# The main loop's patch transforms: once per two steps with 512 columns, in place of once per step with 256

## The reference

```
xn     = layernorm(x)                                 # 16 channels
hidden = xn @ w_hidden                                # 192 channels
qkv    = conv3x3(hidden, w_qkv, SAME)                 # 192 channels, split into q, k, v of 64
out    = irfft2(rfft2(patches(q)) * rfft2(patches(k)))  # patches of 8 x 8 pixels
out    = v * layernorm(out)                           # over 64 channels
out    = out @ w_out + x                              # 16 channels
```

## Time and profile before

| | |
|---|---|
| median of three runs | 236.66 us (236.47 to 239.24) |
| the profiled execution's own time | 237.58 us |
| its span, first to last instruction | 235.8 us |
| PE busy | 219.5 us (93%) |
| DVE busy | 159.4 us (68%) |
| ACT busy | 133.8 us (57%) |
| POOL busy | 76.9 us (33%) |
| mean granted TensorE clock | 0.993 |

### The profile page before, as it was taken

One profiled execution on the slowest core, in us unless ns is written; L12 is line 12 of the kernel. 1 busy time (PEld: TensorE's weight loads), 2 busy tenths in 40 slices (PEclk: granted clock), 3 DMA queues, 4 the chain that ended last, 5 costly groups with the idle time before them and its releaser, 6 DMA issues.

```text
span 235.8 us, 4977 instructions
## 1 busy us (share of the span) xinstructions
PE 219.5 (93%) x1926; PEld 144.1 (61%) x1926; DVE 159.4 (68%) x301; ACT 133.8 (57%) x286; POOL 76.9 (33%) x70
## 2 busy tenths in 40 slices
PE   7989999895989899779999999999999999999983
PEld 3359434772447557268676676767676777767561
DVE  3995123567743983646489978678786889677793
ACT  3366475323174754344678666667667576766533
POOL 1635500012300000000051766426654364549730
PEclk9999999999799999999999999999999999999999
DMA  6920000000000018989997479999950000000001
GB/s 215 329 70 7 16 8 4 20 3 0 4 0 0 0 64 190 223 193 194 201 197 151 141 137 191 182 179 202 191 118 0 3 24 25 0 1 3 22 0 67
DMA packets 22647, 21.07 MB, mean 89 GB/s; under 512 B 1898, under 2 KB 21242, under 8 KB 22522
## 3 DMA queue, kind: packets, MB, share of 16 engines
q1 hardware_dynamic: 22352, 20.62, 43.0%
q10 hardware_dynamic: 272, 0.14, 0.3%
HBM read 16.58 MB, written 4.02 MB: 87 GB/s over the span
## 4 chain that ended last, share of the span: by engine, by line
PE 68%; DVE 16%; ACT 6%; DMA 6%; issue 2%; SPq 1%; DVEq 0%; ACTq 0%
PE psum L1229 22%; PE psum L1240 13%; PE psum L1250 7%; PE psum L1102 5%; PE psum L1175 4%; PE psum L1260 3%; DMA arena<-parts 3%; DVE xc L781 2%; PE psum L1080 2%; DVE sq L793 2%; PE psum L1090 2%; PE psum L1063 2%; DMA parts<-tr 2%; DVE st L787 2%; PE psum L1286 2%
## 5 line engine op out<-in xcount | busy, mean ns | idle before, releaser
L1229 PE MATMUL psum<-wc,tile 128*128 128x192 f32 (+1 forms) x384 | 59.4, 305 | 3.5 <-ACT tile L378 1.9
L1229 PEld LDWEIGHTS psum<-wc,tile 128*128 128x128 f32 (+1 forms) x384 | 51.4, 159 | 13.7 <-issue 7.8
L557 POOL TENSOR_TENSOR zp<-zp,ln 128x512 f32<-128x512 f32 x14 | 17.8, 1274 | 100.6 <-DVE zp L937 100.6
L916 DVE TENSOR_TENSOR arena<-psum,arena 128x512 f32<-128x512 f32 x32 | 22.1, 691 | 27.5 <-ACT arena L716 27.2
L378 DVE COPY tile<-arena 128x256 f32<-128x256 f32 x64 | 25.1, 435 | 2.1 <-DMA arena<-parts 2.1
L1175 PE MATMUL psum<-arena,wdw 102*128 102x512 f32 x48 | 23.5, 631 | 0.9 <-ACT arena L339 0.9
L716 ACT COPY arena<-psum 128x512 f32<-128x512 f32 x32 | 18.8, 586 | 9.0 <-PE psum L1240 9.0
L1250 PE MATMUL psum<-arena,km 128*64 128x256 f32 x128 | 20.9, 405 | 0.2 <-DVE arena L916 0.2
L709 ACT COPY spec<-psum 128x768 f32<-128x768 f32 x16 | 12.8, 799 | 12.7 <-PE psum L1229 12.7
L558 POOL TENSOR_TENSOR zp<-zp,ln 128x512 f32<-128x512 f32 x14 | 17.8, 1271 | 1.1
L1240 PE MATMUL psum<-spec,km 64*128 64x256 f32 x128 | 18.2, 402 | 0.0
(11 more groups left out here) (129 smaller groups left out, 373.1 us busy)
## 6 DMA issues: line engine op xcount, KB each, us to landing
arena<-padded SPq DMA_DIRECT2D x16, 393.0 KB, 9.8
arena<-parts SPq DMA_DIRECT2D x16, 196.5 KB, 9.7
arena<-padded SPq DMA_DIRECT2D x8, 262.0 KB, 10.4
parts<-tr SPq DMA_DIRECT2D x12, 115.5 KB
wq<-w_qkv SPq DMA_DIRECT2D x1, 1296.0 KB, 11.9
padded<-tr SPq DMA_DIRECT2D x4, 264.0 KB, 3.9
arena<-parts SPq DMA_DIRECT2D x8, 131.0 KB, 9.6
out<-xt SPq DMA_DIRECT2D x8, 128.0 KB, 1.7
```

The source lines that it names most:

```text
L557: pool_link(pool.tensor_tensor(y, y, along(0), ALU.mult))
L916: dve.tensor_tensor(pr[:, m % 2], f_half(m, 0), kh[:, m % 2], ALU.mult).then_inc(prod, 1)
L1229: last = mm(bank[a][:, HID * h:HID * h + HID], stationary[:, n % 2, 2 * h + a, :], moving[:, :], start=first and h == 0, stop=not first, s ...
```

## The change

The transforms forward and back are done once a pair, with 512 columns a matmul. `forward(i)` fills four banks, 2 to 5: first the two k matmuls, with a signal of their own (`fk_mm`), then the two q matmuls (`f_mm`). `k_out` copies 1024 columns and `product` multiplies 1024, both with one buffer in place of two. The inverse has bank 6 alone in place of banks 4 and 5 by turns, and `turn` and `unit` share bank 7. The last pair stays in halves, as before, on banks 0 to 3. The orders of all three loops are written anew over pairs s: PE runs convolution 2s, forward of pair s-1, unit, convolution 2s+1, turn, inverse of pair s-1. On DVE `finish` stands right behind `o_scale`, with the next `gather` and then `o_sum` behind it; on ACT `o_square` stands ahead of `conv_out(2s)`, and `k_out` behind it. The parts of the second half of the images are split at s = 1 and 2.

```diff
-        kh = spare[:, 0:1024].rearrange("p (i q n) -> p i q n", i=2, q=2)
-        pr = spare[:, 1024:2048].rearrange("p (i q n) -> p i q n", i=2, q=2)
+        kh, pr = spare[:, 0:1024], spare[:, 1024:2048]
...
         def o_bank(i):
-            return bank[4 + i % 2]
+            return bank[6 if i < 15 else 4]
...
         def yt_bank(i):
-            return bank[6 if i < 15 else 0]
+            return bank[7 if i < 15 else 0]
...
-            def k_out(m):
-                act.wait_ge(f_mm, m + 1)
-                if m >= 2:
-                    act.wait_ge(prod, m - 1)
-                act.copy(kh[:, m % 2], f_half(m, 1)).then_inc(k_ev, 1)
+            def k_out(i):
+                act.wait_ge(fk_mm, i + 1)
+                if i >= 1:
+                    act.wait_ge(prod, i)
+                act.copy(kh, psum[:, 2048:3072]).then_inc(k_ev, 1)
...
             gather9(0)
-            for n in range(32):
-                if n + 1 < 32:
-                    gather9(n + 1)
-                if n in (6, 7):
+            for s in range(16):
+                gather9(2 * s + 1)
+                if s >= 2:
+                    o_square(s - 2)
+                conv_out(2 * s)
+                if s >= 1:
+                    k_out(s - 1)
+                if s in (1, 2):
                     for b2 in range(2):
-                        part(1, n - 6, b2)
...
+                        part(1, s - 1, b2)
+                if s < 15:
+                    gather9(2 * s + 2)
+                if s >= 2:
+                    root(s - 2)
+                u = unit_after(s - 4)
+                if u is not None:
                     unit_out(u)
+                conv_out(2 * s + 1)
+                if 3 <= s < 15:
+                    turned(s - 3)
+
+            k_out_half(0)
+            k_out_half(1)
...
+            def product(i):
+                dve.wait_ge(k_ev, i + 1)
+                dve.wait_ge(f_mm, i + 1)
+                if i >= 1:
+                    dve.wait_ge(o_mm, i)
+                dve.tensor_tensor(pr, psum[:, 1024:2048], kh, ALU.mult).then_inc(prod, 1)
...
             gather(0)
...
+            for s in range(16):
+                gather(2 * s + 1)
+                if s == 1:
+                    bordered(1)
+                if s >= 2:
+                    o_sum(s - 2)
+                    o_centre(s - 2)
+                if s == 0:
                     normalise(2, 1, xc[:, 1])
...
+                if s < 15:
+                    gather(2 * s + 2)
+                if s >= 2:
+                    o_variance(s - 2)
+                if s >= 1:
+                    product(s - 1)
+                if s in (1, 2):
+                    split(1, s - 1)
+                if s >= 2:
+                    o_scale(s - 2, o_norm)
+                u = unit_after(s - 4)
+                if u is not None and u < 5:
                     finish(u)
...
+            def forward(i):
+                pe.wait_ge(qkv_ev, 2 * i + 2)
+                pe.wait_ge(x2_done, 8)
+                if i >= 1:
+                    pe.wait_ge(prod, i)
+                for part, name, signal in ((1, "fk", fk_mm), (0, "fq", f_mm)):
+                    for q in range(2):
+                        rows = slice(64 * q, 64 * q + 64)
+                        src = qkv[i % 4][rows, :, :, CH * part:CH * part + CH].rearrange("p e t c -> p (e t) c")
+                        last = mm(bank[2 + 2 * part + q][:, :], const(name)[rows], src, start=True, stop=True)
+                    last.then_inc(signal, 1)
...
+            def inverse(i):
+                pe.wait_ge(prod, i + 1)
+                if i == 0:
+                    pe.wait_ge(tr_ev, 4)
+                else:
+                    pe.wait_ge(o_centred, i)
                 for q in range(2):
-                    last = mm(o_bank(i)[64 * q:64 * q + 64, 256 * e:256 * e + 256], const("inv4"), pr[:, m % 2, q, :], start=True, stop=True)
+                    last = mm(o_bank(i)[64 * q:64 * q + 64, :], const("inv4"), pr[:, 512 * q:512 * q + 512], start=True, stop=True)
+                last.then_inc(o_mm, 1)
...
                     pe.wait_ge(yt_ev, i)
+                    if unit_after(i - 1) is not None:
+                        pe.wait_ge(pj_ev, unit_after(i - 1) + 1)
...
+            for s in range(16):
+                conv(2 * s)
+                if s >= 1:
+                    forward(s - 1)
+                u = unit_after(s - 4)
+                if u is not None:
+                    unit(u)
+                if s == 1:
                     channel_major(1)
...
+                conv(2 * s + 1)
+                if 3 <= s < 15:
+                    turn(s - 3)
+                if s >= 1:
+                    inverse(s - 1)
```

More of the change, by code:

```diff
@@ L300, in two_blocks @@
         tiled, qkv_mm, qkv_ev = sem("tiled"), sem("qkv_mm"), sem("qkv_ev")
-        f_mm, k_ev, prod, o_mm = sem("f_mm"), sem("k_ev"), sem("prod"), sem("o_mm")
+        fk_mm, f_mm, k_ev, prod, o_mm = sem("fk_mm"), sem("f_mm"), sem("k_ev"), sem("prod"), sem("o_mm")
         o_summed, o_centred, o_squared, o_var, o_sd, o_norm, gated = map(sem, "o_summed o_centred o_squared o_var o_sd o_norm gated".split())
@@ L710, in conv_out, with k_out_half @@
                          psum[:, 0:1024].rearrange("p (a n) -> p a n", a=2)[:, :, 0:2 * HID]).then_inc(qkv_ev, 1)
-            def k_out(m):
-                act.wait_ge(f_mm, m + 1)
-                if m >= 2:
-                    act.wait_ge(prod, m - 1)
-                act.copy(kh[:, m % 2], f_half(m, 1)).then_inc(k_ev, 1)
+            def k_out(i):
[3 more added lines that the diff above has]
+                act.copy(kh, psum[:, 2048:3072]).then_inc(k_ev, 1)
+            def k_out_half(e):
+                act.wait_ge(f_mm, 16 + e)
+                act.wait_ge(prod, 15)
+                act.copy(half_of(kh, e), half_banks(e)[:, :, 1, :]).then_inc(k_ev, 1)
             def o_square(i):
@@ L910, in per_group, with product_half @@
                 return a.rearrange("p (t a) -> p t a", a=1).broadcast_to([P, 8, CH])
[L912 to L916, removed]
+            def product(i):
[4 more added lines that the diff above has]
+                dve.tensor_tensor(pr, psum[:, 1024:2048], kh, ALU.mult).then_inc(prod, 1)
+            def product_half(e):
+                dve.wait_ge(k_ev, 16 + e)
+                dve.wait_ge(f_mm, 16 + e)
+                dve.wait_ge(o_mm, 15)
+                dve.tensor_tensor(half_of(pr, e), half_banks(e)[:, :, 0, :], half_of(kh, e), ALU.mult).then_inc(prod, 1)
             def o_sum(i):
-                dve.wait_ge(o_mm, 2 * i + 2)
+                dve.wait_ge(o_mm, i + 1 if i < 15 else 17)
                 dve.tensor_reduce(out=stat[:, i % 2, 0, :], in_=groups(o_bank(i)), axis=AX.X, op=ALU.add).then_inc(o_summed, 1)
@@ L951, in _ @@
             gather(0)
[L952 to L958, removed]
-                    normalise(2, 1, xc[:, 1])
[L960 to L973, removed]
+            for s in range(16):
[6 more added lines that the diff above has]
+                if s == 0:
+                    normalise(2, 1, xc[:, 1])
+                if s < 15:
[10 more added lines that the diff above has]
+                if u is not None and u < 5:
                     finish(u)
-            product(31)
+            o_sum(14)
             o_centre(14)
+            product_half(0)
+            product_half(1)
             o_sum(15)
@@ L1231, in conv, with forward_half @@
                 last.then_inc(qkv_mm, 1)
[L1233 to L1236, removed]
+            def forward(i):
[9 more added lines that the diff above has]
+                    last.then_inc(signal, 1)
+            def forward_half(e):
+                pe.wait_ge(qkv_ev, 31 + e)
+                pe.wait_ge(prod, 15)
                 for part, name in enumerate(("fq", "fk")):
@@ L1239, in forward, with inverse_half @@
                         rows = slice(64 * q, 64 * q + 64)
-                        last = mm(f_banks(m)[q][:, 256 * part:256 * part + 256], const(name)[rows],
-                                  qkv[m // 2 % 4][rows, m % 2, :, CH * part:CH * part + CH], start=True, stop=True)
+                        last = mm(half_banks(e)[:, q, part, :], const(name)[rows], qkv[3][rows, e, :, CH * part:CH * part + CH], start=True, stop=True)
                 last.then_inc(f_mm, 1)
[L1244 to L1248, removed]
-                for q in range(2):
-                    last = mm(o_bank(i)[64 * q:64 * q + 64, 256 * e:256 * e + 256], const("inv4"), pr[:, m % 2, q, :], start=True, stop=True)
+            def inverse(i):
[4 more added lines that the diff above has]
+                    pe.wait_ge(o_centred, i)
+                for q in range(2):
+                    last = mm(o_bank(i)[64 * q:64 * q + 64, :], const("inv4"), pr[:, 512 * q:512 * q + 512], start=True, stop=True)
+                last.then_inc(o_mm, 1)
+            def inverse_half(e):
+                pe.wait_ge(prod, 16 + e)
+                for q in range(2):
```

(13 more changed lines are left out.)

21 lines of the change are left out of this document (4 added, 17 removed).

## The result

The changed kernel takes 241.91 us (median of four runs, 240.10 to 242.22) against 237.29 for the kernel before in the same comparison: the ratio is 1.018, 95% interval 1.013 to 1.023. It is slower by less than 2%, with an interval that excludes no change. The forecast was 240.2 in a range of 233.0 to 242.6. The profiled execution took 242.22 us, its span is 240.4 us. Some executions of each kernel here are slower at a lower mean granted clock: the medians take in all executions, the ratios leave those out.

The account below looks back on a forecast made before the run. PE bounded the kernel before; after the change, the ring through DVE and ACT in most pairs. Loop +2.7, start +0.3, end +0.5 us on 237.58 gave 241.1 profiled, 240.2 by the median, range 233.0 to 242.6.

Parts of the forecast that it names:

- PE's gain: Main loop on PE: fewer changes of shape between groups make a pair 7.02 us, or 7.60 with a unit, 0.3 less.
- The ring: Waits through DVE and ACT from one product to the next: 7.27 us a pair, 8.98 with `finish`.
- The long instructions: Copy and product of 1024 columns on ACT and DVE, drawn from shorter ones: 1.01 and 1.22 us.
- The held add: The add of `finish` on DVE, taken as held by POOL's first gate instruction: begins at 2.04, over at 2.40 us.
- The sum: Whole kernel: +2.7 us for steps 8 to 30, +0.3 at the start, +0.5 at the end, together +3.5.
- The end: After the loop: halves take 0.25 us longer, the last finish delays the last whole product by 0 to 0.8: +0.5.
- The median: Whole time: 241.1 us for the profiled execution, which ran 0.9 over the median before, so 240.2.
- The clock: PE's granted clock: 9 tenths or more in every slice, 2.4 GHz throughout, so no term is about it.
- the first (add not held): Rival on DVE: copies are held beside POOL, the add of `finish` is not; 233.7 us, chance 0.33.
- The second (a ring longer than its rows): Rival in the loop: the ring takes 0.2 us more in each pair, 243 us, over 2% slower; chance 0.13.
- the third (no gain on PE): Rival on PE: pairs stay at 7.4 and 7.95 us; 241.5 with the add held, 237.3 without; chance 0.06.

Follow-up runs that it names:

- e5_both: The changed kernel with DVE's order product, finish, gather, `o_scale`, and `o_square` behind `conv_out(2s)` on ACT: 233.63 us, ratio 0.981 to the kernel before.

## Why the prediction was right, point by point

- **PE's gain**: 0.3 us a pair was forecast. With the ring no longer the bound the pairs are 7.02 and 7.59 against 7.34 and 7.91, the groups as in the sum. Shown, and that it comes from the grouping is shown for the forward transform.
- **The ring**: forecast 7.27 and 8.98 us, measured 7.25 and 8.87. That it is the bound was shown by shortening it: by the add alone (8.06 us, about 8.1 expected), by the copy of 768 columns alone (8.16, 8.17 expected), and by add and gather together, where PE's 7.02 and 7.59 became the bound as expected. That 7.27 came so close owes a little to luck: the stretch from `o_scale` to the end of the gather took 2.20 us (forecast 2.12), the step from `o_sum` to `o_centre` 0.70 (0.78). The prediction's words that "the single buffers and the new order close" it were half wrong: the order does it without the SBUF buffers.
- **The long instructions**: `k_out` 1.02 us (forecast 1.01), the product 1.22 (1.22). Two points had been drawn on to a third, and held.
- **The held add**: the one price that no row had. Taken at its upper end, because the add is like the held copies and unlike what kept its time. Measured 1.24 us, five times out of five beside POOL, 0.43 free. The trace agrees here with the rule that the prediction took from the Trainium skill, "SBUF — State Buffer", section "Who interferes with whom": the add has two SBUF inputs. What the hold costs is not its length, though: 0 in the kernel before, 3.2 us of the stretch in the changed one.
- **The sum**: the spans differ by 240.4 - 235.8 = 4.6 us, forecast 3.5. Steps 8 to 30 take 2.4 us more (forecast 2.7; its 84.3 us for before took one start from the chain and one from the timeline, with both from the timeline it is 84.1). Step 8 starts 0.35 us later (forecast 0.3), and that is luck: from the first convolution to step 8 the loop gained 0.3 us, and the first convolution itself came 0.7 us later, 0.4 of it ahead of the warming matmuls and the rest in the wait for loads, both in code that the change doesn't touch.
- **The end** is the term that was mis-sized: 0.5 forecast, 1.8 measured, all of it up to the last inverse, which starts 11.79 us after convolution 30 in place of 9.96. The prediction counted 0.25 for the halves and what the last finish leaves of the slack ahead of the last inverse. It left out that `conv_out(30)` stands behind the square in the ring, so that convolution 31 waits 0.90 us for it. It starts 5.29 us after convolution 30, against 3.94 before; the other 0.45 is the new order, with a forward transform of 1.92 us and a unit between the two. The last 0.5 comes behind convolution 31. With finish and gather ahead that wait is gone and convolution 31 starts 4.31 us after convolution 30.
- **The median**: 241.91 lies 1.7 us over the forecast. The sum gives 1.1 of it. The rest is that the profiled execution of the changed kernel lies 0.3 us over its median, not 0.9 as in the kernel before.
- **The clock**: the prediction reads "9 tenths or more in every slice", but one slice in the earlier trace rows stands at 7, from about 59 to 62 us. It lies ahead of the main loop, and no term of the sum rests on it.
- **The rivals**: the first (add not held) fell by the add's length. The second (a ring longer than its rows) and the third (no gain on PE) fell by 7.25 us and 1.92 us.

## What to carry to other kernels

When two short steps are merged into a long one with one place in each queue, follow the ring from that step back to itself through every in-order queue, and add up all that stands in it; a ring can bound a loop though each of its engines waits in it: DVE was busy for 72% of the span and 91% of the stretch here, ACT for 60% of the stretch. Price an instruction by what runs beside it on the neighbour that can hold it, as POOL held these copies and adds on DVE, and put it where that neighbour is idle, or where the hold is outside the ring: here a few lines moved on DVE turned +1.8% into -1.3%. Idle time ahead of a step is cover: an edit that spends it makes the holds behind it cost.

## What the hardware showed that was not expected

The granted clock at the loop's start is not the same in each execution. Where PE had been idle for 3.70 us ahead of the first convolution, in the profile of `e5_both`, the clock was down over the first two convolutions, and they took 2.81 and 3.54 us in place of 1.87 (columns as above):

```profile
100.00:104.00 4.00, 2.81 (x12) 2.26 (x12) 3.19 (x10) 1.35 (x5) 0.00 (x0) 0.67 0.75 176
104.00:108.00 4.00, 3.54 (x12) 3.01 (x12) 0.00 (x0) 0.70 (x4) 0.00 (x0) 0.50 1.13 193
```

With the forward transforms in halves it fell as well, after 2.87 us of idle time, and the first three convolutions took 3.54 us each. With finish and gather ahead it fell after 1.90 us, for one convolution (3.25 us). In the eight other profiles it stayed at the upper level, after 0.81 to 2.87 us of idle time. What decides it is open. In a single execution it cost up to 5 us: from the first convolution to that of step 3 it took 15.51 us with the forward transforms in halves, 10.34 with more warming.

The clock also falls ahead of the loop, where the code of these kernels is the same but for the number of warming matmuls: in the profile before from about 59 to 62 us, in the changed kernel from about 17 to 21 us, with finish ahead of `o_scale` and with more warming at both places. The first convolution starts at 103.84 us with finish ahead of `o_scale`, and at 99.67 with two buffers, whose clock is 1.00 throughout. This is the reason to compare such kernels by a stretch inside the loop as well.
